# A binarised convolution block with a gated expert network: image pairs loaded in halves, expert weights in portions, and the router's sums read between two outputs

## The reference, cut to what matters

```python
# block 1: sign of the channel-normalised image, 3x3 convolution with binarised weights, batch norm, clip
x = x + clip(batchnorm(conv(sign(layernorm_channels(x)), binarised(conv_weight))), -1, 1)
# block 2: every point of every image is a token of 64 features; 8 experts of three 64x64 layers
t = tokens(x)                                   # (32, 3136, 64)
xn = layernorm(t)
w = softmax(mean(xn, axis=0) @ Wr + br)         # router: one gate per point, over 8 experts
h = relu(bn1(einsum('bfd,edh->bfeh', xn, W1) + b1))
h = relu(bn2(einsum('bfeh,ehk->bfek', h, W2) + b2))
y = einsum('bfeh,ehd->bfed', h, Wo) + bo
t = t + einsum('bfed,fe->bfd', y, w)
```

## Time and profile before

| what | value |
|---|---|
| time, median of 3 runs | 1359.81 us (1358.64 to 1362.91) |
| the profiled execution's own time | 1365.09 us |
| its span | 1363.3 us |
| PE busy | 1297.5 us (95%) |
| DVE, ACT, POOL busy | 869.4, 850.7, 525.2 us |
| mean granted TensorE clock | 0.987 |
| moved by transfers | 112.49 MB, 83 GB/s over the span |

### The profile page before, as it was taken

The page is one execution under the profiler, slowest core; times in us unless marked ns, Lnnn a source line. Parts: engine busy times, 40 slices in busy tenths (PEclk is TensorE's granted clock), DMA queues, the critical chain, the costliest instruction groups (busy, mean ns, idle before and its releaser), DMA issues.

```text
span 1363.3 us, 36385 instructions
## 1 busy us (share of the span) xinstructions
PE 1297.5 (95%) x14692; PEld 662.3 (49%) x14692; DVE 869.4 (64%) x1580; ACT 850.7 (62%) x1122; POOL 525.2 (39%) x468
## 2 busy tenths in 40 slices
PE   5899959999999999999999999999999999999997
PEld 3677724545444345545444444544444555543453
DVE  4344646676667666676765676666666666767665
ACT  4567656666656666666666666666666666666543
POOL 0515003433434424444334435334444344443341
PEclk9999969999999999999999999999999999999999
DMA  8988703442434424343423334424334233344121
GB/s 182 177 182 180 146 0 69 83 86 47 84 70 80 83 44 87 71 78 81 90 57 73 71 76 83 86 46 83 76 76 83 65 67 70 76 85 87 29 62 28
DMA packets 255856, 112.49 MB, mean 83 GB/s; under 512 B 240520, under 2 KB 244192, under 8 KB 255712
## 3 DMA queue, kind: packets, MB, share of 16 engines
q1 hardware_dynamic: 254448, 108.85, 39.5%
q0 software_dynamic: 1264, 1.61, 0.7%
HBM read 84.25 MB, written 26.17 MB: 81 GB/s over the span
## 4 chain that ended last, share of the span: by engine, by line
PE 93%; DMA 3%; issue 2%; DVE 1%; SPq 1%; ACT 1%; POOLq 0%; DVEq 0%
PE ps L603 27%; PE ps L563 26%; PE ps L587 26%; PE ps L524 6%; PE ps L623 3%; DMA xa<-in_x 3%; PE ps L509 3%; PE ps L631 2%; SPq L268 1%; PE ps L643 0%; PE ps L709 0%; PE ps L698 0%; DVE xin L1003 0%; DVE xc L1065 0%; PE ps L660 0%
## 5 line engine op out<-in xcount | busy, mean ns | idle before, releaser
L982 DVE SCALAR_TENSOR_TENSOR v<-ps,negb,wb 128x448 f32<-128x448 f32 x896 | 570.8, 678 | 350.1 <-PE ps L587 342.9
L790 ACT ACTIVATE h<-ps,bias 128x896 f32<-128x896 f32 x448 | 451.0, 1007 | 306.5 <-PE ps L563 306.0
L603 PE MATMUL ps<-v,wo 64*64 64x448 f32 x3584 | 470.7, 543 | 10.7 <-issue 9.9
L563 PE MATMUL ps<-xc,w 64*64 64x448 f32 x3584 | 468.9, 542 | 5.9 <-issue 5.7
L587 PE MATMUL ps<-h,w 64*64 64x448 f32 x3584 | 466.7, 542 | 4.4 <-issue 3.3
L466 POOL TENSOR_TENSOR o<-o,upper 128x448 f32<-128x448 f32 x112 | 127.6, 1140 | 422.2 <-DVE o L992 422.2
L587 PEld LDWEIGHTS ps<-h,w 64*64 64x64 f32 x3584 | 173.9, 133 | 191.2 <-issue 170.6
L603 PEld LDWEIGHTS ps<-v,wo 64*64 64x64 f32 x3584 | 169.7, 133 | 176.5 <-issue 161.1
L563 PEld LDWEIGHTS ps<-xc,w 64*64 64x64 f32 x3584 | 166.4, 132 | 177.8 <-issue 165.8
L458 POOL TENSOR_TENSOR o<-xin,gconst 128x448 f32<-128x448 f32 x112 | 126.4, 1150 | 248.0 <-DMA out<-o 93.3
L436 POOL TENSOR_TENSOR xc<-xc,spread 128x896 f32<-128x896 f32 x54 | 112.4, 2092 | 64.7 <-DMA spread<-rs_rows 64.6
(11 more groups left out here) (163 smaller groups left out, 634.8 us busy)
## 6 DMA issues: line engine op xcount, KB each, us to landing
xa<-in_x SPq DMA_DIRECT2D x64, 392.0 KB, 6.9
xin<-in_x SPq DMA_DIRECT2D x112, 224.0 KB, 5.0
out<-o SPq DMA_DIRECT2D x224, 112.0 KB, 2.7
spread<-rs_rows SPq DMA_DIRECT2D x108, 224.0 KB, 4.2
wb<-gate_rows SPq DMA_DIRECT2D x54, 112.0 KB, 2.8
rs_rows<-rs SPq DMA_DIRECT2D x54, 7.0 KB
gate_rows<-wT SPq DMA_DIRECT2D x54, 1.8 KB
rows<-in_L_ffn_g POOLq DMA_DIRECT2D x2, 256.0 KB, 10.0
```

The costliest lines, as they stand in the source:

```text
L563: last = mm(ps[64 * two:64 * two + 64, L1_BANKS + ab, 0:NG], w1[half, P * q + C * two:P * q + C * two + C], xc[half, s, g // 2, ab ^ (g % ...
L603: last = mm(ps[64 * par:64 * par + 64, ACC_BANKS + low, 0:NG], wo[rows_, 2 * Q + d, :], v[rows_, u % 2, par ^ (g % 2), d, :], start=(Q == ...
L790: A(h[:, u % 2, i], ps[:, L1_BANKS:L1_BANKS + 2, 0:NG], ACT.Relu, bias=bias[:, 0, q:q + 1]).then_inc(h_done[i], 1)
L982: last = V.scalar_tensor_tensor(out=v[:, u % 2, ab, d, :].rearrange("p (b w) -> p b w", w=W), in0=ps[:, L2_BANKS[ab] + d, 0:NG].rearrange( ...
```

## The change

`load_images` brings each pair in two halves j of 14 rows each: eight transfers of 196 KB in runs of 3136 bytes, each half with a semaphore of its own. Half j of pair m is issued when groups 0 to 2j + 1 of pair m - 2 are centred. `centre_images` waits for half 0 at group 0 and for half 1 at group 2. POOL's weights go out in portions: the four `rows` behind pairs 2, 3, 4 and 5, all of `cols` directly behind the fourth of these, `wraw` and `wo` in halves behind pairs 6 and 7, with `gb` and `brb`, and the rest behind pair 8. ACT's `fold_roots` moves from behind pair 8 to behind pair 11. In the loop DVE's two logits additions move from behind `layer2_out(k, s, 6, 0)` to between its two instructions.

```diff
-        s_xa = [sem(f"s_xa{i}") for i in range(XRING)]
+        s_xa = [[sem(f"s_xa{i}_{j}") for j in range(2)] for i in range(XRING)]
...
+        LOGITS_BETWEEN = -1
...
                 def load_images(m):
-                    if m >= XRING:
-                        sp.wait_ge(a_centred, GA * (m - XRING) + GA)
-                    for n in range(2):
-                        for h in range(2):
-                            xb = x[2 * m + (n ^ h), :, RP * h:RP * h + RP, :].rearrange("c k w -> c (k w)")
-                            sp.dma_start(xa[64 * h:64 * h + 64, xa_slot(m), n].rearrange("p g e -> p (g e)"), xb).then_inc(s_xa[xa_slot(m)], 16)
+                    for j in range(2):
+                        if m >= XRING:
+                            sp.wait_ge(a_centred, GA * (m - XRING) + GA // 2 * j + GA // 2)
+                        for n in range(2):
+                            for h in range(2):
+                                top = RP * h + RP // 2 * j
+                                xb = x[2 * m + (n ^ h), :, top:top + RP // 2, :].rearrange("c k w -> c (k w)")
+                                sp.dma_start(xa[64 * h:64 * h + 64, xa_slot(m), n, GA // 2 * j:GA // 2 * j + GA // 2].rearrange("p g e -> p (g e)"),
+                                             xb).then_inc(s_xa[xa_slot(m)][j], 16)
...
                 dma = pool.dma_start
-                pool.wait_ge(a_centred, GA * 3)
+                def behind(m):
+                    pool.wait_ge(a_centred, GA * m + GA)
                 for i, vec in enumerate((g1, v1, g2, v2)):
+                    behind(2 + i)
                     dma(rows[:, i, :], ...)
...
                 for hi in range(2):
+                    behind(6 + hi)
                     dma(wraw[64 * hi:64 * hi + 64], ...)
...
+                behind(8)
                 dma(w2raw[:], ...)
...
                 def centre_images(m, turn, slot, g):
-                    if g == 0:
-                        pe.wait_ge(s_xa[slot], N_XA * turn + N_XA)
+                    if g % (GA // 2) == 0:
+                        pe.wait_ge(s_xa[slot][g // (GA // 2)], N_XA * turn + N_XA)
...
-                    if m == TWOS // 2:
+                    if m == TWOS - 5:
                         fold_roots()
...
                     for d in range(2):
                         ... V.scalar_tensor_tensor(out=v[...], ...)
+                        if d == 0 and ab == 0 and u == UNITS - 2 and k + 1 < RP:
+                            prep(STEADY, k + 1, 1 - s, LOGITS_BETWEEN)
                     last.then_inc(v_done[ab], 1)
...
-                    if h == at.logits:
+                    if h == (LOGITS_BETWEEN if at is STEADY else at.logits):
                         dve.wait_ge(logits_done, q + 2)
```

## The result

The changed kernel takes 1344.4 us (median of 4 runs, 1343.3 to 1350.1) against 1360.3, a ratio of 0.9874 with a 95% interval of 0.9851 to 0.9898. It is 16 us faster by the medians. Its profiled execution took 1343.4 us with a span of 1341.6.

A forecast was written before the change was run, and what follows sets the result against it. The prediction took PE, busy 95% of the span, as the bound. Stage A's 12.6 us (3.6 + 9.0) and the loop's 2.8 sum to 15.4, taking the median from 1359.8 to 1344.4 us, range 1338 to 1353.

The forecast's parts named there:

- Start: Start of stage A: with half pairs PE's regular rhythm begins at 17.4 instead of 21.0 us, -3.6 us.
- Waits: Stage A behind the start: halves and portions remove PE's waits for `xa` and the slow clock, -9.0 us.
- Cost of the halves: Image loads in stage A: 64 more transfers on SP and shorter runs cost nothing, 0 us.
- Fold: POOL's fold, moved later by 13.5 us, ends at 146 and stays hidden inside stage A, 0 us.
- Way over: The stretch behind stage A, hanging on the last statistics, moves along with stage A's end, unchanged.
- Logits: Loop: earlier additions end PE's 0.30 us wait at `layer2(6, 1)`; 0.12 kept in 23 steps, -2.8 us.
- Sum: Whole kernel: 12.6 us from stage A and 2.8 from the loop make 15.4 us faster.
- the full logits gain: Rival, loop: PE alone holds the `layer1` behind the turn, so the loop gives 6.9 us: 1340; chance 0.10.
- the weights in the way: Rival, stage A: weights still stretch pair loads, 5 to 8 us of waits stay: 1350 to 1353; chance 0.17.
- the gain taken back: Rival, behind stage A: the way over waits for something unmoved, most of 12.6 us goes: 1357; chance 0.08.
- slower transfers: Rival, image loads: runs of 3136 bytes cost as much as 6272, stage A follows DMA: about 1440; chance 0.05.

The follow-up runs named there:

- Experiment 2: Kernel before with pairs loaded in halves alone, weights, roots and logits as before: 1349.5 us against 1360.4, ratio 0.9927.
- experiment 3: Kernel before with weights in portions and roots behind pair 11 alone, whole pairs, logits as before: 1360.4 us against 1360.4, ratio 0.9998.
- Experiment 6: Changed kernel, but both halves of a pair requested only when all four groups of pair m - 2 are centred: 1343.1 us, 0.9875 of the kernel before.
- Experiment 7: Changed kernel with pairs in quarters, sixteen transfers of 98 KB, released and awaited group by group: 1368.0 us against 1360.1 for the kernel before, ratio 1.0053.
- the mixed version: Changed kernel without the gate's maximum and subtraction, halves of pairs 2 and 3 alone requested after the whole pair two before: 1335.4 us, 0.9814 of the kernel before.
- experiment 1: Kernel before with the logits edit alone: 1355.4 us against 1360.4, ratio 0.9964.

## Why the prediction was right, point by point

**Start** (-3.6): measured -4.4, pair 1 centred from 16.67 instead of 21.04. The two landings I set at 13.7 and 17.4 came at 13.0 and 16.4. The mechanism was right: two of pair 0's centrings are started before its second half lands, and the last sign (16.2) and the first half of pair 1 come nearly together. In other profiles with halves the trace names the sign and not the landing as the last to come.

**Waits** (-9.0): all three behind the start went, as did the slow clock at 53. But the stops "issue" grew from 0.79 us before to 3.0. The term nets -7.0, and stage A gives 11.4 instead of 12.6. Experiment 2 shows that the halves alone remove the waits, experiment 3 that the portions alone remove none of the time. I had booked the term to both. Experiment 6 narrows it further: I had laid the lead to the earlier request (14.5 us instead of 10.2), but with the old request and the weights in portions only 0.9 of the 9.0 came back. So awaiting half a pair is enough there, and the early request, which I counted as pure gain, went with the larger stops, for which I had no term.

**Cost of the halves** (0): no loss in bytes moved, as the earlier trace rows let expect: from 6 to 13 us DMA moves 242 GB/s at a share of 1.03, before 234 at 1.04. Experiment 7 puts the limit one step further, at SP's issue. The estimate by the Trainium skill, page "DMA: Bandwidth & Descriptors", parts "Anatomy of one DMA" and "Measured", would have had the halves cost more than 100 us if nothing overlapped. Both parts give their figures for transfers issued by GpSimd, which the prediction left out, while SP issues these. The trace does not agree with the estimate for loads issued this closely.

**Fold** (0): ends at 147.6, predicted 146; hidden.

**Way over** (unchanged): 1.2 us longer by the second `layer1` (38.2 behind stage A's end instead of 37.0). Of it 0.76 is one variance step on PE that ran at 1.2 instead of 2.4 GHz (0.96 us at a granted clock of 1.00 before, 1.72 at 0.50 after).

**Logits** (-2.8, bounds 0 and -6.9): the mechanism held in each place, `layer2(6, 1)` at 0.75, the exponential 0.12 earlier, `layer1` held by `layer1_out`. The term was sized too small. I took the step at 526 us as typical and 23 steps; in steps whose take-out starts later, `layer2(6, 1)` stood up to 1.26 us behind, and there the edit gives more. By the traces 0.15 to 0.17 over 27 steps, 4.1 to 4.6 us; timed, 5.0 (2.3 to 7.5).

**Sum**: -11.4 + 1.2 - 4.4 = -14.6 by the traces against -15.9 measured and -15.4 predicted. The sum lands this well partly because the stops, the longer way over and the larger logits and start terms offset each other, and that the median came out at the very 1344.4 of the forecast is luck: the four executions lie between 1343.3 and 1350.1. The two profiles differ by 21.7; the profiled execution of before stood 5 us above its median, with the longest loop of all kernels traced here.

**Rivals**: the full logits gain is refuted by the 2.46 us where 2.3 would be free, the weights in the way by the changed kernel's trace, where no start waits for `xa` behind 16.67, the gain taken back by the sum, slower transfers by the 242 GB/s.

## What to carry to other kernels

A ring of two buffers that are filled whole gives a transfer little lead. To await half of one buys an earlier start, and together with the release by halves a lead that swallowed the burst of other traffic, which made spreading it unnecessary here. The release by halves is to be measured by itself: with the traffic spread it brought nothing that the times show, and the kernels that had it with full halves had stops of PE of 2.7 us or more, which those without it had not (last section). Stop splitting where the issuing queue's time a buffer (number of transfers times 0.6 us, and its waits) comes near the consumer's period. When an operand is read earlier for a waiting engine, look at what stands next in the queue of the third engine: here the exponential ahead of a take-out kept half of the gain, and a shorter chain to it released most of the rest (0.11 us more a step).

## What the runs showed of the hardware that was not expected

PE's stops in stage A go with the transfers of queue 8, "instruction", 16 KB each. The stops of stage A shown above stand at the same two places of PE's program in every kernel, behind the 19th matmul of the fourth convolution and behind the 10th of the seventh, and the first two transfers of that queue can be laid beside them. In the 14 profiles of this document these are 28 passes. In 14 of them PE stands, and each time it goes on 1.3 to 1.5 us after the end of the transfer; in the other 14 the transfer had ended 1.3 to 7.0 us before PE came to the place. In the changed kernel (its second profile) the second transfer runs from 31.75 to 33.04 us and PE stands from 31.5 to 34.45; in the mixed version it runs from 25.07 to 26.40, and PE passes the place at 30.46 without a stop. The windows from 30 to 35 us, the changed kernel first, then the mixed version:

```profile
30.00:35.00 5.00, 2.35 (x51) 1.56 (x47) 1.57 (x4) 1.73 (x3) 0.00 (x0) 1.00 1.01 233
```

```profile
30.00:35.00 5.00, 5.00 (x108) 4.06 (x104) 2.21 (x5) 3.75 (x6) 0.79 (x1) 1.00 1.04 237
```

DMA is full in both, at 233 and 237 GB/s, so a full DMA while PE is at the place is not enough; it matters when the code came. Kernels with full halves and the early release for pairs 2 and 3 had stops of 2.7 to 4.2 us in all (five profiles), those with the later release, the mixed one and the one with half the bytes had none (four profiles). What makes the transfer late is open, since the trace shows when code is moved and not when it was asked for. It goes with the amount of images under way: from PE's pass of the first place to the start of the second transfer it takes 5.5 to 6.5 us in the six profiles that have 1.6 MB or more of images issued and not yet landed at that pass, and 4.4 at most in the eight with 1.0 MB or less. The quarters, with DMA 0.6 busy, and the portions alone had none either; the stage A of the kernel before had 0.8 and 0.9 us of them in two profiles and 3.4 in a third (experiment 1).
